# Causal mask products with 64x64 identity tiles, one set for both diagonal blocks of a unit

## The reference

```python
scores = jnp.einsum('bshd,bthd->bhst', q / jnp.sqrt(Hd), k)
future = jnp.triu(jnp.ones((S, S), dtype=bool), 1)
scores = jnp.where(future[None, None, :, :], jnp.finfo(scores.dtype).min, scores)
attn = jax.nn.softmax(scores, axis=-1)
ctx = jnp.einsum('bhst,bthd->bshd', attn, v)
```

## Time and profile before

| | us |
|---|---|
| time, median of 3 runs | 490.84 (489.36 to 491.09) |
| span of the profiled execution | 1523.4 |
| time of the profiled execution beside its span | none recorded apart from it |
| PE busy in it | 1509.8 |
| DVE busy | 405.0 |
| ACT busy | 370.9 |
| POOL busy | 184.6 |

### The profile page before, as it was taken

The page is one execution under the profiler, slowest core; times in us unless marked ns, Lnnn a source line. Parts: engine busy times, 40 slices in busy tenths (PEclk is TensorE's granted clock), DMA queues, the critical chain, the costliest instruction groups (busy, mean ns, idle before and its releaser), DMA issues.

```text
span 1523.4 us, 12413 instructions
## 1 busy us (share of the span) xinstructions
PE 1509.8 (99%) x4432; PEld 813.3 (53%) x4432; DVE 405.0 (27%) x1147; ACT 370.9 (24%) x879; POOL 184.6 (12%) x349
## 2 busy tenths in 40 slices
PE   7999999999999999999999999999999999999998
PEld 4545654433453454557553444556543745784786
DVE  2433223333222333212223222122221231111112
ACT  2223222221322232221122223222212232313111
POOL 4200012000301101101001001111011122011111
DMA  5110000100000000000010000100000000000000
GB/s 145 31 43 1 9 6 22 34 18 7 1 21 12 11 12 11 1 1 5 1 32 1 1 0 3 27 1 1 4 4 0 1 0 0 0 1 1 0 0 14
DMA packets 27185, 18.40 MB, mean 12 GB/s; under 512 B 8217, under 2 KB 26773, under 8 KB 26997
## 3 DMA queue, kind: packets, MB, share of 16 engines
q1 hardware_dynamic: 23413, 15.44, 3.8%
q10 hardware_dynamic: 3712, 2.17, 0.6%
HBM read 5.58 MB, written 1.05 MB: 4 GB/s over the span
## 4 chain that ended last, share of the span: by engine, by line
PE 99%; DVE 0%; ACT 0%; POOL 0%; issue 0%; POOLq 0%; ACTq 0%; DVEq 0%
PE psum L1064 14%; PE psum L1179 9%; PE psum L1389 8%; PE psum L1325 7%; PE psum L1412 7%; PE psum L1120 6%; PE psum L1147 6%; PE psum L1423 5%; PE psum L1169 4%; PE psum L1166 3%; PE psum L1099 3%; PE psum L1434 3%; PE psum L1126 3%; PE psum L1153 3%; PE psum L1281 2%; PE psum L1207 2%
## 5 line engine op out<-in xcount | busy, mean ns | idle before, releaser
L1557 ACT ACTIVATE EX<-psum 128x1024 f32<-128x1024 f32 (+1 forms) x128 | 122.6, 971 | 155.4 <-PE psum L1153 109.9
L1179 PE MATMUL psum<-EX,V 128*32 128x256 f32 (+3 forms) x512 | 133.4, 1284 | 0.0
L1120 PE MATMUL psum<-K,Q 64*128 64x154 bf16 (+4 forms) x512 | 129.9, 595 | 0.5 <-DVE nmax L1813 0.5
L1147 PE MATMUL psum<-Q,K 64*128 64x512 bf16 (+3 forms) x320 | 126.2, 803 | 0.0
L1818 DVE TENSOR_REDUCE nmax<-psum 128x2 f32<-128x768 f32 (+1 forms) x96 | 79.9, 866 | 130.8 <-PE psum L1126 130.4
L1813 DVE TENSOR_REDUCE nmax<-psum 128x4 f32<-128x616 f32 (+1 forms) x80 | 68.5, 882 | 126.9 <-PE psum L1120 100.2
L1389 PE MATMUL psum<-GP,xT 128*128 128x308 f32 x96 | 102.0, 1264 | 0.0
L1412 PEld LDWEIGHTS psum<-VM,REST 128*128 128x128 f32 x192 | 80.4, 555 | 5.2 <-issue 3.2
L1412 PE MATMUL psum<-VM,REST 128*128 128x128 f32 x192 | 82.5, 662 | 0.0
L1325 PE MATMUL psum<-ew,xT 128*128 128x512 f32 x48 | 81.0, 1932 | 0.0
L1179 PEld LDWEIGHTS psum<-EX,V 128*32 128x32 f32 x512 | 36.5, 217 | 79.7 <-issue 75.7
(11 more groups left out here) (345 smaller groups left out, 2042.0 us busy)
## 6 DMA issues: line engine op xcount, KB each, us to landing
Q<-xparts SPq DMA_DIRECT2D x24, 128.0 KB
Q<-parts SPq DMA_DIRECT2D x21, 128.0 KB
K<-parts SPq DMA_DIRECT2D x21, 128.0 KB
X<-in_x SPq DMA_DIRECT2D x4, 256.0 KB, 3.0
Q<-in_L_xattn_Wkv SPq DMA_DIRECT2D x1, 1024.0 KB, 7.3
K<-xkparts SPq DMA_DIRECT2D x24, 38.5 KB
out<-XB_rest SPq DMA_DIRECT2D x6, 128.0 KB, 1.8
Q<-in_L_xattn_Wq SPq DMA_DIRECT2D x1, 512.0 KB, 4.4
```

The costliest lines, as they stand in the source:

```text
L1120: last = mm(to[:, r, at:at + n], Q6[a][p, b % 2, 2 * g + jj, P * q:P * q + P], K6[a][p, b % 2, 2 * g + jj, 0:n], start=True, stop=bool(a))
L1147: last = mm(to[:, r, at:at + n], K6[a][p, b % 2, 2 * g + jj, P * k:P * k + P], Q6[a][p, b % 2, 2 * g + jj, P * k:S], start=True, stop=bool(a))
L1179: last = mm(to[32 * h:32 * h + 32, P * k:S], V[:, k, 4 * g + h, :], EX[:, ex_slot(b, a, g, u) + h % 2, at:at + n], start=k == PV_ORDER[0], ...
L1557: drains(nc.scalar.activation(dst, src, ACT.Exp), key)
```

## The change

`SELF_T_PIECES` gets other pairs: block 3 of a slot now stands in front and block 1 behind it at column 128, so that the two diagonal blocks of a unit begin at a fixed distance. The mask products move behind the loop over the pieces. Each one uses a 64 x 64 identity (`ident2[p, 0, 0:TILE]`) and writes one half `e` of the partitions; the new helper `diagonals` gives the output of both diagonal blocks as one access with a stride, and the mask is read twice by a broadcast. A unit has four mask products, whether it has one piece or two; they have 128 and 64 columns with one piece, 256 and 128 with two. The flag `start` is set only on the first piece of a bank.

```diff
--- before.py
+++ after.py
@@ -68,7 +68,7 @@
 SELF_PIECES = [[(0, 0, 3)], [(0, 1, 3)], [(0, 0, 2), (384, 0, 0)], [(0, 1, 2), (384, 1, 0)],
                [(0, 0, 1), (256, 1, 1)]]
 
-SELF_T_PIECES = [[(0, 0, 0)], [(0, 1, 0)], [(0, 0, 1), (384, 0, 3)], [(0, 1, 1), (384, 1, 3)],
+SELF_T_PIECES = [[(0, 0, 0)], [(0, 1, 0)], [(0, 0, 3), (P, 0, 1)], [(0, 1, 3), (P, 1, 1)],
                  [(0, 0, 2), (256, 1, 2)]]
 
 PV_ORDER = 0, 1, 3, 2
@@ -1105,6 +1105,13 @@
                     pe.wait_ge(qk_normed, 2 * b + w if b else 1)
                 to_features((b, "qkT", w), qkn[:, :, w, :])
 
+            def diagonals(to, starts, cols):
+
+                n = starts[-1] - starts[0] if len(starts) > 1 else P
+                at = starts[0] // P * P % n
+                return to[:, starts[0] - at:starts[0] - at + n * len(starts)].rearrange(
+                    "p (j k) -> p j k", k=n)[:, :, at + cols.start:at + cols.stop]
+
             def scores(b, a, g, u):
                 if a == b == u == g == 0:
                     pe.wait_ge(consts_ready, 1)
@@ -1118,13 +1125,15 @@
                     for r in R:
                         p = slice(TILE * r, TILE * r + TILE)
                         last = mm(to[:, r, at:at + n], Q6[a][p, b % 2, 2 * g + jj, P * q:P * q + P],
-                                  K6[a][p, b % 2, 2 * g + jj, 0:n], start=True, stop=bool(a))
-                    for e in (() if a else (1, 0)):
-
-                        for r in R:
-                            p = slice(TILE * r, TILE * r + TILE)
-                            last = mm(to[:, r, at + n - P + TILE * e:at + n], ident2[p, e, :],
-                                      maskS[p, e, TILE * e:P], start=False, stop=e == 0)
+                                  K6[a][p, b % 2, 2 * g + jj, 0:n], start=at == 0 or bool(a), stop=bool(a))
+                for e in (() if a else R):
+
+                    cols = slice(TILE * e, P)
+                    for r in R:
+                        p, half = [slice(TILE * i, TILE * i + TILE) for i in (r, e)]
+                        last = mm(diagonals(to[half, r, :], [at + P * q for at, _, q in PIECES[a][u]], cols),
+                                  ident2[p, 0, 0:TILE], maskS[p, e:e + 1, cols].to_broadcast([TILE, len(PIECES[a][u]), cols.stop - cols.start]),
+                                  start=False, stop=True)
                 fills_(last, key)
 
             def scores_T(b, a, g, u):
@@ -1145,13 +1154,15 @@
                     for r in R:
                         p = slice(TILE * r, TILE * r + TILE)
                         last = mm(to[:, r, at:at + n], K6[a][p, b % 2, 2 * g + jj, P * k:P * k + P],
-                                  Q6[a][p, b % 2, 2 * g + jj, P * k:S], start=True, stop=bool(a))
-                    for e in (() if a else R):
-
-                        for r in R:
-                            p = slice(TILE * r, TILE * r + TILE)
-                            last = mm(to[:, r, at:at + TILE * (e + 1)], ident2[p, e, :],
-                                      maskT[p, e, 0:TILE * (e + 1)], start=False, stop=e == 1)
+                                  Q6[a][p, b % 2, 2 * g + jj, P * k:S], start=at == 0 or bool(a), stop=bool(a))
+                for e in (() if a else R):
+
+                    cols = slice(0, TILE * e + TILE)
+                    for r in R:
+                        p, half = [slice(TILE * i, TILE * i + TILE) for i in (r, e)]
+                        last = mm(diagonals(to[half, r, :], [at for at, _, _ in SELF_T_PIECES[u]], cols),
+                                  ident2[p, 0, 0:TILE], maskT[p, e:e + 1, cols].to_broadcast([TILE, len(SELF_T_PIECES[u]), cols.stop - cols.start]),
+                                  start=False, stop=True)
                 fills_(last, key)
 
             def values(b, a, g):
```

## The result

The changed kernel takes 505.47 us (median of 4 runs, 505.02 to 506.75) against 490.66 us of the kernel before on the same chip: ratio 1.0296, 95% interval 1.0269 to 1.0323. It is 14.8 us slower. The forecast was 514.

What follows compares the result with a forecast made beforehand. PE was taken to lead by little in the timed runs, DVE close behind. 490.84 + 41.6 for shape changes - 6.8 for mask columns - 11.7 hidden gave 514 us, with 8 in 10 runs from 484 to 542.

Steps and rivals of the forecast that it cites:

- Price of a change: Each added switch of tile shape on PE costs 0.157 us (bounds 0 and 0.25); 265 of them, 41.6 us.
- Hidden part: DVE's lead in the trace's first 200 us covers 11.7 us of the added PE work.
- Rival 1: Narrowing masks from 128 to 64 columns is no shape change; only columns count: 484 us, chance 0.12.
- Rival 2: Timed runs keep the profile's balance of stops, changes cost nothing, saved masks count: 482 us, chance 0.07.
- Rival 3: DVE, busy 405.0 of 490.84 us, hides all added PE work: 491 us, chance 0.09.
- Rival 4: Each change costs the full 0.25 us way out, none returned: 538 us, 550 with nothing hidden; chance 0.12.
- Rival 5: The 64-column masks save no columns: 521 us; counted within the forecast's 0.60, no chance of its own.
- (a): Sign in the trace: 640 mask products of shape 64*64.
- (b): Sign: a unit's first mask 0.1 to 0.25 us late, its load not ahead; next unit's scores likewise.
- (d): Sign: a unit's four masks begin within some ns of each other, or not.
- (e): Sign: DVE idles longer before L1818.
- (c): Sign: two units in a row each longer by about 0.3 us less the masks' saving, if PE is at full pace.

Runs made afterwards that it cites:

- experiment 5: Changed kernel with only the wider half's mask products issued, two 64x64 tiles a unit instead of four: 504.59 us, ratio 1.0291.
- experiment 6: Kernel of experiment 2 with only the wider half's mask products issued, two a unit, 64x128 identity tile: 487.5 us, ratio 0.9937.
- experiment 2: Changed kernel with 64x128 identity tiles as before, one merged set of masks per unit, no added shape changes: 489.97 us, ratio 0.9978.
- experiment 4: Changed kernel with self scores also made of 64x64 tiles, four products instead of two, one shape per unit: 489.55 us, ratio 0.9956.
- experiment 3: Kernel before with 64x64 identity tiles alone, a set of masks for each block as before: 528.55 us, ratio 1.0744.
- experiment 7: Changed kernel with all self mask products left out: 487.16 us, ratio 0.9925.

## Why the prediction was right in sign and 8.5 us too high

*PE bounds, DVE follows.* Right: 458.1 us of PE in a span of 488.0. But its size was wrong. I had divided PE's 1509.8 us of the earlier trace rows by the 3.93 of the bf16 pairs of the earlier trace rows and got 384; the profile at the timed pace gives 458.1, a factor of 3.30. The pairs' factor does not hold for the other products. With it falls the test of the price by room (384 + 45 = 429 "possible", 456 "barely so"): PE is in fact busy for 458. And that the clock was granted, from which I read that the array stood still, rests on the 1.000 that is no measurement.

*Count of changes.* 265 forecast, 263 found.

*Price of a change.* This is the term that was mis-sized: 0.157 us, from single products between two shapes, against 0.107 by experiments 5 and 6 (263 x 0.107 = 28.1 us instead of 41.6), or about 0.09 once the lower clock of the narrow profile is taken off. A visit has a way in and a way out, 0.09 and 0.12 us, two changes. I had taken the lone visit's surplus for one. Taken for two it gives 0.065 to 0.08, too low: at the array's slow pace these rows could not carry the number. That it came within a factor of two is luck, two errors the opposite way; the bounds of 0 and 0.25 held it.

*Masks' columns.* 6.8 us forecast for side-by-side tiles, 6.0 measured on PE. But I took them off the time in full, where 2.5 us arrives (experiments 2 and 6).

*Hidden part.* 11.7 us forecast from DVE's lead in the earlier trace rows; the stages' windows show 6.2, of it 5.5 before 132 us, so the place was right and the lead too large, for the reason of the first point: with 458 us of work PE left less idle time than with 384.

*The sum again.* 28.1 of changes, 6.8 of columns (6.0 by experiment), 6.2 hidden: 490.7 + 28.1 - 6.8 - 6.2 = 505.8, beside 505.47. My changes were 13.5 us too dear and my hidden part 5.5 too large, the other way; that leaves 8.0 of the miss of 8.5. The close fit proves little: the 6.2 are taken from the very spans that the sum is compared with, and the 28.1 hold some 3.5 us of low clock. The forecast had no term for the clock, which by experiment 4's first stage is worth up to about 2.8 of the 14.8 us.

*Rivals.* Rival 1, no price for the narrow shape: experiment 4 against the changed kernel, and 5 against 6. Rival 2, the balance of the profile: the changed kernel's masks start late and the time rises. Its and my span of 1495 us can't be tried, as that pace did not return. Rival 3, DVE hides everything: it hid 6.2 us; in experiment 3's third stage nothing. Rival 4, 0.25 each: 0.107. Rival 5, no columns saved: experiment 5. The marks (a), (b), (d) and (e) are seen: 320 products a line; masks 0.09 us late with their load not ahead; two products as long as four; DVE's idle time 3.1 to 9.1. Mark (c), 0.3 us a unit less the masks' saving, is 0.21 less 0.06: 0.40 to 0.55.

The Trainium skill, "TensorEngine Tiling (Array Packing)", section Key Properties, says that a change of tiling mode drains the engine. The runs agree as far as they can show it: across a change the masks start 0.32 us after the scores where 0.23 do without one, and their load does not run ahead. They add that the column width alone is such a change: experiments 5 and 6 keep 64 rows and differ only in 64 or 128 columns.

## What to carry to other kernels

Count the changes of tile shape along PE's order before making a tile smaller: here each costs about 0.09 us of PE on average and up to 0.12, some 210 to 290 columns' worth at full clock, and a mask of 64 to 256 columns can't earn two of them back. If the smaller tile is wanted, give its neighbours the same shape (experiment 4), since more and smaller products in one shape were free here. And ask on which side of the knee the kernel sits: removing PE work gave less than half of its size (2.5 of 6.0 us in experiment 6 against 2; 5.6 of 13.7 in the second and third stage of experiment 7), adding it cost nearly all of it (20.6 of 23.2 us in experiment 3), so one factor for both is wrong. Last, compare the granted clock of two profiles before dividing a difference of busy time by a count.

## What was not expected of the hardware

- One profiled execution of the kernel had PE at 3.3 times its usual busy time, and no later one did. The 1.000 given as its clock was no sign of health: the page has no PEclk line. A profile whose span is three times the timed median should be taken again before any duration is read from it.
- Four 64x64 tiles with four different quarters of the array start within some ns of each other, and cost what the longest does.
- The early low clock (1.2 GHz from 28 to 36 us) came in full in five of the six profiles with narrow masks, and at most partly in the five others. What in the narrow masks brings it stays open.
